# Recommender user vectors on one core: more row dots on VectorE in tiles 2 to 6, a later gather, resized fill products

## The reference

```python
decay = exp(-alpha * hist_age_hours) * maskf
mean_hist = (hist_items * maskf[..., None]).sum(1) / (maskf.sum(1, keepdims=True) + 1e-06)
q = mean_hist @ Wq.T
k = einsum('btd,ed->bte', hist_items, Wk); v = einsum('btd,ed->bte', hist_items, Wv)
scores = einsum('bd,btd->bt', q, k) * scale + log(decay + 1e-12)
attn = softmax(where(hist_mask, scores, -inf))
long_term = einsum('bt,btd->bd', attn, v)
short_term = (hist_items * lk[..., None]).sum(1) / denom      # five items ahead of position cnt
g = sigmoid(stack([mean_pop, mean_rec]) @ gate_w.T + gate_b)
user = g * short_term + (1.0 - g) * long_term
return layernorm(user) * ln_gamma + ln_beta
```

## Time and profile before

| | us |
|---|---|
| median of 3 runs | 175.87 |
| lowest and highest | 175.72, 178.6 |
| the profiled execution | 176.9 |
| its span, first to last instruction | 175.1 |

### The profile page before, as it was taken

The page is one execution under the profiler, slowest core; times in us unless marked ns, Lnnn a source line. Parts: engine busy times, 40 slices in busy tenths (PEclk is TensorE's granted clock), DMA queues, the critical chain, the costliest instruction groups (busy, mean ns, idle before and its releaser), DMA issues. The chain is left out here.

```text
span 175.1 us, 8178 instructions
## 1 busy us (share of the span) xinstructions
PE 147.1 (84%) x2811; PEld 113.6 (65%) x2811; DVE 153.0 (87%) x1289; ACT 122.2 (70%) x714; POOL 143.8 (82%) x110
## 2 busy tenths in 40 slices
PE   5766558777679999999998998999998999696780
PEld 5745446666465777877776775877785887364550
DVE  4589849797387899999999999999999999999843
ACT  2021657775385989897988889887889898877420
POOL 5748869889996998999999999999999996975101
PEclk9999996999999999999999999999999999999997
DMA  4799999999999989999999999999999940200000
GB/s 102 269 414 416 253 411 405 406 398 405 416 429 412 362 324 393 408 428 430 407 413 422 416 398 407 413 400 399 415 427 409 371 168 9 50 32 0 19 0 15
DMA packets 8008, 55.48 MB, mean 317 GB/s; under 512 B 2080, under 2 KB 3360, under 8 KB 4000
## 3 DMA queue, kind: packets, MB, share of 16 engines
q1 hardware_dynamic: 7152, 53.59, 77.2%
q0 software_dynamic: 576, 1.33, 2.3%
q10 hardware_dynamic: 240, 0.05, 0.2%
HBM read 54.70 MB, written 0.26 MB: 314 GB/s over the span
## 5 line engine op out<-in xcount | busy, mean ns | idle before, releaser
L969 DVE SCALAR_TENSOR_TENSOR junk_v<-x,ps_query 128x128 f32<-128x128 f32 x548 | 122.0, 279 | 9.6 <-ACT query L660 9.5
L626 ACT ACTIVATE gprod<-gprod 128x128 f32<-128x128 f32 x252 | 74.4, 302 | 11.7 <-POOL gprod L357 11.4
L357 POOL TENSOR_TENSOR gprod<-x,query 128x1024 f32<-128x1024 f32 (+1 forms) x32 | 75.0, 2343 | 8.5 <-ACT query L660 6.0
L457 PE MATMUL ps_acc<-x,mblk 128*16 128x128 f32 x1600 | 56.7, 278 | 6.7 <-DMA x<-in_r_hist_items_dram 6.1
L465 PE MATMUL ps_acc<-x,pblk 128*32 128x256 f32 x768 | 51.6, 381 | 7.9 <-POOL pblk L345 4.8
L457 PEld LDWEIGHTS ps_acc<-x,mblk 128*16 128x16 f32 x1600 | 45.9, 98 | 10.2 <-issue 7.3
L626 ACT ACTIVATION_READ_ACCUMULATOR gprod<-gprod 128x1 f32 x252 | 48.6, 193 | 0.0
L969 DVE DVE_READ_ACCUMULATOR junk_v<-x,ps_query 128x1 f32 x548 | 45.0, 82 | 0.0
L465 PEld LDWEIGHTS ps_acc<-x,pblk 128*32 128x32 f32 x768 | 27.0, 109 | 20.9 <-issue 5.6
L345 POOL TENSOR_TENSOR pblk<-own,ex 128x800 f32<-128x800 f32 (+1 forms) x17 | 24.3, 1432 | 3.8 <-ACT ex L671 3.7
L334 POOL TENSOR_TENSOR mblk<-own,mask_f 128x800 f32<-128x800 f32 (+1 forms) x17 | 25.0, 1471 | 0.2
(11 more groups left out here) (117 smaller groups left out, 134.0 us busy)
## 6 DMA issues: line engine op xcount, KB each, us to landing
x<-in_r_hist_items_dram SPq DMA_DIRECT2D x31, 1600.0 KB, 10.3
x<-in_r_hist_items_dram SPq DMA_DIRECT2D x1, 832.0 KB, 7.9
x<-in_r_hist_items_dram SPq DMA_DIRECT2D x1, 768.0 KB, 6.3
decay_s<-in_r_hist_age_hours_dram SPq DMA_DIRECT2D x4, 100.0 KB, 13.8
out_dram<-y SPq DMA_DIRECT2D x4, 64.0 KB, 5.0
mask_u<-in_r_hist_mask_dram SPq DMA_DIRECT2D x1, 100.0 KB, 7.1
wq<-in_L_rec_Wq_dram SPq DMA_DIRECT2D x1, 64.0 KB, 7.3
wk<-in_L_rec_Wk_dram SPq DMA_DIRECT2D x1, 64.0 KB, 7.4
```

What stands on the lines that cost most here:

```text
L357: nc.gpsimd.tensor_tensor(gprod[:, t, 0:k * D].rearrange("p (r d) -> p r d", d=D), rows(at(s, t), ROWS - k, ROWS), query[:, s % 2, t, :].u ...
L457: ins = nc.tensor.matmul(dst[c:c + TU, 0:D], blk[:, s % 2, t, m, :], x[:, at(s, t), m * D:(m + 1) * D], start=(m < CG), stop=(m >= ROWS - CG))
L626: ins = nc.scalar.activation(src, src, ACT.Copy, accum_out=score[:, s % 2, t, at_row:at_row + 1])
L969: ins = V.scalar_tensor_tensor(out=junk_v[:, t, r, :], in0=x[:, at(s, t), r * D:(r + 1) * D], scalar=1.0, in1=c_query[t], op0=ALU.mult, op ...
```

## The change

VectorE makes 21 dots instead of 17 in tiles 2 to 6 and GpSimd multiplies 4 rows there instead of 8, so ScalarE sums 4. `sum_products` takes its bounds from `dots_of`, and the second part of tile 6 in slot 9 falls away. VectorE's loop over the even tiles of a pair takes its length from `dots_of` as well. `gather(0)` moves from the end of GpSimd's slot 4 to the end of its slot 6. The fill products of slots 0 to 5 become 6, 8, 7, 2, 3 and 3 instead of 4 each.

```diff
-DOTS, DOTS_LAST = 17, 21
+DOTS, DOTS_LAST, MORE_DOTS = 17, 21, range(2, 7)
 GPROD = ROWS - DOTS
...
-BUSY_FIRST, BUSY_LEAD, BUSY_LAST = 13, 4, {NTILE - 4: 6}
+BUSY_FIRST, BUSY_LEAD, BUSY_LAST = 13, (6, 8, 7, 2, 3, 3), {NTILE - 4: 6}
...
         def dots_of(n):
 
-            return DOTS_LAST if n == LAST_TILE else DOTS
+            return DOTS_LAST if n == LAST_TILE or n in MORE_DOTS else DOTS
...
-                if n == NGROUP:
+                if n == LEAD - 1:
                     gather(0)
...
-                if n <= 5:
-                    keep_busy(ps_group[:, D:2 * D], BUSY_LEAD)
+                if n < len(BUSY_LEAD):
+                    keep_busy(ps_group[:, D:2 * D], BUSY_LEAD[n])
...
                 if tile(n - 1):
-                    sum_products(n - 1, 0, GPROD)
+                    sum_products(n - 1, 0, ROWS - dots_of(n - 1))
...
-                if n > LEAD + 1 and n <= NTILE and tile(n - 3):
+                if n > LEAD + 1 and n <= NTILE and tile(n - 3) and dots_of(n - 3) == DOTS:
                     sum_products(n - 3, ROWS_AHEAD, GPROD)
...
-                for i in range(DOTS):
+                for i in range(dots_of(s * PAIR)):
```

## The result

| | before | changed |
|---|---|---|
| median, us (20 runs each, same chip) | 176.34 | 174.91 |
| lowest and highest | 175.12, 179.74 | 174.1, 177.85 |
| ratio, 95% interval | | 0.993, 0.990 to 0.996 |
| profiled execution, its span | 176.9, 175.1 | 177.07, 175.3 |

The change makes the kernel 0.7% faster, 1.2 us by the ratio, where 3.06 us were forecast. Executions of both kernels lie on two levels some 3 us apart: a ratio compares those on the lower one, of kernels on the same chip, while the profiled 177.07 of the changed kernel, 3.0 us above its fastest, is on the upper one.

The account below looks back on a forecast made before the run. VectorE was taken as the bound, gapless behind 62 us but waiting for queries in the first 60; -7.23 us idle and +4.17 us of dots gave -3.06 from 175.87, so 172.8 us (forecast 172.4 to 173.5, range 172.0 to 175.0).

Parts of the forecast that it names:

- The lead: VectorE from tile 2 to tile 8: with no waits left, tile 8 starts at 57.10 instead of 60.16, 3.06 us earlier.
- -7.23 and +4.17: VectorE, tile 2 to tile 8: 7.23 us of idle time removed, 4.17 us of work added by 20 more dots.
- The dots at 0.209 us: VectorE, tiles 2 to 6: each added dot costs 0.209 us, four cost 0.83 us a tile, 20 cost 4.17 us.
- Rival (c): VectorE's dots cost 0.36 us each, so 20 take 7.2 us, the whole idle time: 175.8 us, chance 0.02.
- The products, the gather and the block matrix: GpSimd: four-row products take 1.28 us, the moved gather costs nothing, the first block matrix starts at 38.8 instead of 43.12.
- Tile 3 at full clock: TensorE's masked sums of tile 3 take 1.69 us instead of 3.12, with slot 2's fills raised; otherwise 0.3 us lost.
- (a): Late loads hold the queries of tiles 7 and 8, taking 0.7 to 2 us: 173.5 to 174.9 us, chance 0.19.
- (b): VectorE's 3.03 us wait ahead of tile 6 stays, so nothing is gained: 175.8 us, chance 0.05.
- (d): TensorE falls to half clock from slot 6, 2.8 us a slot: 177.1 us for two, 179.9 from the third, chance 0.06.
- Rival (e): Whole kernel more than 2% faster, needing 3.5 us, if earlier runs idle more than the profiled one: chance 0.12.
- VectorE ... has no gap behind 62 us: VectorE, 62 to 158 us, busy 95.59 of 96.00: an earlier arrival, at most 3.06 us, carries to the end.
- The fills at nothing: TensorE, slots 0 and 1: added fills cost between nothing and 1.59 us, taken as nothing because they end in load waits.

Follow-up runs that it names:

- after_p2: The changed kernel unaltered, run again for another profile and ratio: median 178.44 us, ratio to before 1.001 (0.997 to 1.005).
- after_p3: The changed kernel unaltered, a single further profile: 94.91 us between VectorE's fourth and fifteenth row of a pair's maxima (tile 8 to tile 30).
- after_p5: The changed kernel unaltered, run again in the third set: median 178.43 us, too few executions for a ratio.
- dots_gather2: First repeat of the changed kernel with the old four fills in each of slots 0 to 5: median 174.42 us, ratio to before 0.986 (0.980 to 0.992).
- pe_more: The changed kernel with two more fills (0.53 us) ahead of the weighted sums in each of slots 12 to 33: ratio 1.043 (1.033 to 1.052).
- sums13_before: The kernel before with masked sums over 13 of the 25 rows, 26 matmul records a tile instead of 50: median 176.27 us.
- before_p2: The kernel before unaltered, a second profile: 95.48 us between VectorE's fourth and fifteenth row of a pair's maxima (tile 8 to tile 30).
- first8: The changed kernel with 8 instead of 13 fills ahead of the first slot: 175.63 us, ratio to before 0.993 (0.990 to 0.996).
- dots_gather3: Second repeat of the changed kernel with the old four fills in each of slots 0 to 5: median 176.68 us, too few executions for a ratio.
- sums13_after: The changed kernel with masked sums over 13 of the 25 rows, 26 matmul records a tile instead of 50: median 173.91 us.
- first18: The changed kernel with four fills in each of slots 0 to 5 and 18 instead of 13 ahead of them: 176.54 us, ratio to before 0.997 (0.991 to 1.002).
- again_after: The changed kernel unaltered, run once more for a second profile: median 179.48 us, ratio to before 1.009 (1.002 to 1.015).
- fills24: The changed kernel with fills 6, 8, 7, 1, 1, 1 in slots 0 to 5, 24 in all as before: ratio to before 0.9996 (0.989 to 1.011).
- only_dots: The kernel before with the 21 dots and shorter products in tiles 2 to 6 alone: median 179.39 us, ratio to before 1.003 (0.994 to 1.012).

## Why the prediction fell short

**The lead: right.** VectorE had no idle row from 25.57 to 97.38. Tile 8 started 31.74 us after tile 2; forecast were 57.10 - 24.74 = 32.36. There are 568 dots. The sum of -7.23 and +4.17 held, with 0.6 us more gained than it had. The waits for the query fell from 9.5 to 6.5 us and not to 3: the five of the steady stretch are 2.53 of these, and the one ahead of tile 2 is 3.26.

**The dots at 0.209 us: right.** Rival (c) needed 0.36 us a dot; then tile 8 could not have come before 60. The sentence on the DRAIN that stood behind it (the Trainium skill, "VectorE: DVE Perf Modes", section "The DRAIN you can't avoid") does not describe these starts; the same section adds that a next operation that is not held starts earlier, which is what the rows show.

**The products, the gather and the block matrix: right.** GpSimd's rows of the changed kernel:

```profile
38.26 1.29 POOL L357 TENSOR_TENSOR gprod<-x,query 128x512 f32<-128x512 f32 x1
...
39.50 1.55 POOL L345 TENSOR_TENSOR pblk<-own,ex 128x800 f32<-128x800 f32 x1
...
45.88 0.98 POOL L403 DMA_INDIRECT taken<-in_r_hist_items_dram,first_row  x1
46.88 1.56 POOL L345 TENSOR_TENSOR pblk<-own,ex 128x800 f32<-128x800 f32 x1
```

The four-row product took 1.29 us (forecast 1.28) and the block matrix stood at 39.50 instead of 43.12, forecast 38.8. The gather, which costs its 0.98 us behind the product of tile 6, delayed nothing in the lead.

**Tile 3 at full clock: right in this profile.** The row below answers the 3.12 us in the earlier trace rows. In `after_p2`, `after_p3` and `after_p5` the same sums took 2.10 to 2.44 us.

```profile
27.41 1.69 PE L457 MATMUL ps_acc<-x,mblk 128*16 128x128 f32 x50 [0.63 <-DMA x<-in_r_hist_items_dram]
```

The reason given, the three more fills of slot 2, was not needed: `dots_gather2`, with the old four, shows the same.

```profile
26.04 1.69 PE L457 MATMUL ps_acc<-x,mblk 128*16 128x128 f32 x50 [0.68 <-DMA x<-in_r_hist_items_dram]
```

**Rivals (a), (b) and (d): not seen.** No wait stood ahead of tiles 6 to 8, and the granted clock behind 62 us was 1.00. The loads of the steady stretch landed 1.3 to 4.4 us ahead of their masked sums. Rival (e) did not come either.

**Two steps failed.** The first is in the first paragraph: "VectorE ... has no gap behind 62 us, so the end comes earlier by as much as VectorE reaches that point earlier, until something else falls behind it". The condition at its end was tested for one thing alone, the late loads. TensorE's room stood in rival (d) as 4.2 less 3.5 us, 0.7 a slot, and was used for nothing but the half clock. It was built from a few of a slot's items. The earlier trace rows already had the figure: TensorE busy 92.27 of 96.00 us. With 22 to 23 slots in that stretch the 3.7 us left are 0.16 a slot, and `pe_more` measured 0.1. (The agreement is in part luck: busy time is no clean measure of work. `sums13_before` has 524 records fewer in that stretch, which at 1.69 us for 50 is 17.7 us, and is busy only 9.5 us less.) With that the rival "a lead of 3 us is spent on TensorE's pauses" would have had a place and a price.

**The fills at nothing: wrong,** and this is the second step that failed. The prediction says: "Their fills cost between nothing and their own 1.59 us, and I take nothing for them." `dots_gather` differs from the changed kernel in these six counts alone. Its ratios are 0.988 and 0.986 where the changed kernel has 1.001 and 0.995 beside it, so the counts cost 2.3 and 1.6 us by the ratios (0.1 and 1.5 by the medians, 1.8 in the third set). With the old fills the change gives 2.1 to 2.5 us of the 3.06.

Two mechanisms have evidence, and their shares stay open. The first is the fills' own time in the lead. The cover was read from one execution, in which TensorE stood idle for a load ahead of tiles 1, 2 and 3; in `before_p2`, the same kernel, it stood for none of the three. In the first profile of the changed kernel the fills were covered. In four of its six profiles tile 2's sums start at 22.4 to 22.9 us, straight behind the fills; in `dots_gather` and its repeats they start at 21.05 to 21.70, behind half as many. Where tile 2's first dot came before 26 us, the fourth L934 row stands at 61.07 and 61.98 in the changed kernel and at 60.28 and 60.53 in `dots_gather2` and `dots_gather3`. The second mechanism was not thought of at all: ten more records move everything behind them against the grid of instruction blocks. The steady stretch is 95.9 us on average in the six profiles of the changed kernel and 94.9 in the nine with the old grid, 1.0 us more; among executions within 1.5% of the fastest alone it is 0.5. But `first8` has the old grid and the new counts, and it was only 0.25 us under the changed kernel.

**A version that beats both** is `dots_gather`: the dots, the shorter products and the moved gather, with four fills a slot. It was 1.2% and 1.4% faster than before, with the upper ends of the intervals at 0.997 and 0.992, and 0.1 to 1.8 us under the changed kernel by the medians of each of three sets.

## What to carry to other kernels

An engine without a gap bounds a stretch only as far as the others can follow it: before a lead is carried to the end, work out the room a slot of each engine that feeds it, from its busy time in that stretch and not from a list of its larger items, and test it by adding work to that engine. Where the feeding engine has some 0.1 us of room a slot, a gain of more than its slack must be measured with that engine relieved, which also tells a real gain that was given back from one that never was. Work put into gaps is free only as long as the gaps are there: read them in several executions, since the gap for tile 2 was 1.75 us in one execution of before and none in the next. And an instruction inserted anywhere shifts all later ones against the block ends of that engine's instruction stream, so variants that differ in the count of instructions ahead of a stretch are compared over several profiles.

## What the runs showed of the hardware

TensorE paused for its own instructions at fixed places of its stream, every 125.5 matmul records or a multiple, for up to 2.54 us; resumption came 2.17 to 2.69 us after the start of a 16 KB packet of the instruction queue, 80 times in 17 profiles. The longest stood on the fold (2.54 us, `first18`), among the weighted sums (2.26 us, `again_after`) and among the masked sums (2.17 us, `fills24`). With about half the masked sums (`sums13_before`, `sums13_after`) or with 0.53 us of fills added a slot (`pe_more`) none over 0.5 us was left behind 45 us; why is open. How long one gets in a given execution stays open: the same place in the same kernel had 0.55 to 1.81 us.

ScalarE's copies of the sums of tiles 1 and 2 started 0.6 to 2.4 us after TensorE had finished them in ten of the 17 profiles. In `only_dots` the sums ended at 16.6, and nothing on the chip that the profile shows was left to wait for:

```profile
14.86 1.69 PE L457 MATMUL ps_acc<-x,mblk 128*16 128x128 f32 x50 [1.12 <-DMA x<-in_r_hist_items_dram]
...
18.70 0.37 ACT L636 ACTIVATE sums<-ps_acc,rcnt_rows 128x128 f32<-128x128 f32 x1 [5.53 <-remote]
```

In these ten tile 2's first dot stands at 27.7 to 29.8, in the others at 24.6 to 25.6 and, in `first18`, at 26.65, in the kernel before as in the changed one. Most of the scatter between executions of one kernel begins here: `dots_gather` reaches the fourth L934 row at 63.98, its repeats at 60.28 and 60.53, and the spans are 175.0, 172.4 and 172.3 us. Its cause is open.
